# The last routing of a mixture of experts and its first expert chunks, put in another order

## What is computed

```
x = layernorm(x + latent_self_attention(x))        # 16 heads, latent of 72, causal
x = layernorm(x + cross_attention(x, ctx))         # 16 heads of 64, 120 context rows
x = layernorm(x + experts(x) + shared_ffn(x))

scores = softmax(x @ gate_w.T)                     # 16 experts
topk_w, topk_idx = top_k(scores per sequence and expert, cap = 32)
x_tok = x[topk_idx]                                # gather
h = gelu(x_tok @ Wg.T) * (x_tok @ Wu.T)            # per expert, 256 -> 512
out[topk_idx] += (h @ Wd.T) * topk_w               # 512 -> 256, scatter-add
```

## Time and profile before

| what | value |
|---|---|
| runs | 3175.33, 3177.28, 3179.11 us, median 3177.28 |
| profiled execution: span from first to last instruction | 3171.4 us |
| median of the runs less that span | 5.9 us |
| busy share of the span: PE, DVE, ACT, POOL | 97%, 71%, 68%, 50% |
| first transposes of gathered rows, first expert block | 2294 us, 2298 us |
| begin of chunk 2, of chunk 3 | 2350 us, 2367 us |

### The profile page before, as it was taken

How to read it: one execution, slowest core, us unless ns; L and a number is a source line. 1 busy time by engine, 2 the same in 40 slices (tenths; PEclk the granted TensorE clock), 3 DMA queues, 4 the chain that set the end, 5 groups by cost and what they waited for, 6 DMA issues and landing times. The chain is left out here.

```text
span 3171.4 us, 78666 instructions
## 1 busy us (share of the span) xinstructions
PE 3088.7 (97%) x22624; PEld 2900.2 (91%) x22624; DVE 2256.1 (71%) x6566; ACT 2142.4 (68%) x6930; POOL 1581.9 (50%) x2904
## 2 busy tenths in 40 slices
PE   6999999999999998999999999999989999999998
PEld 5999999999999987999999999999868888889998
DVE  6777777777877877778877778787745455544665
ACT  6888888888887877787877877777734444442222
POOL 3666766766676765333333333333446666653000
PEclk8999999999999999999999999999989999999999
DMA  6444444444444440121111111111245444533333
GB/s 181 117 120 125 127 125 121 121 120 122 127 111 111 125 143 24 48 64 45 54 55 45 57 55 44 64 45 48 94 118 119 100 98 101 128 56 85 120 124 106
DMA packets 193684, 300.70 MB, mean 95 GB/s; under 512 B 33856, under 2 KB 134080, under 8 KB 192704
## 3 DMA queue, kind: packets, MB, share of 16 engines
q1 hardware_dynamic: 168768, 262.91, 27.8%
q0 software_dynamic: 24576, 33.57, 6.2%
HBM read 116.02 MB, written 67.11 MB: 58 GB/s over the span
## 5 line engine op out<-in xcount | busy, mean ns | idle before, releaser
L964 POOL TENSOR_SCALAR ca_prob<-ca_prob,ca_inverse 128x120 f32<-128x120 f32 x1024 | 354.6, 365 | 632.5 <-DVE ca_inverse L1268 630.5
L665 ACT ACTIVATE sa_prob<-sa_prob,sa_shift 128x128 f32<-128x128 f32 (+1 forms) x1024 | 453.6, 461 | 2.6 <-DVE sa_shift L718 2.6
L1206 ACT ACTIVATE ca_prob<-bank,ca_shift 128x120 f32<-128x120 f32 x1024 | 353.7, 366 | 6.0 <-DVE ca_shift L1262 3.5
L460 POOL TENSOR_SCALAR sa_prob<-sa_prob,sa_inverse 128x128 f32<-128x128 f32 x512 | 198.5, 388 | 234.5 <-DVE sa_inverse L726 220.4
L718 DVE CUSTOM_DVE_ANT_0 sa_prob<-bank,sa_mask 128x128 f32<-128x128 f32 (+1 forms) x1024 | 304.7, 352 | 6.9 <-PE bank L138 2.7
L136 PE MATMUL bank<-sa_ow,sa_y_hi 128*128 128x256 f32 x1024 | 279.6, 304 | 0.0
L136 PE MATMUL bank<-sa_kvT_a,sa_q 128*128 128x128 f32 (+1 forms) x1024 | 251.7, 281 | 17.7 <-DMA sa_q<-sa_q_tile 17.4
L138 PE MATMUL bank<-sa_kvT_b,sa_q 112*128 112x128 f32 (+1 forms) x1024 | 261.6, 281 | 0.0
L749 DVE TENSOR_TENSOR sa_pT_lo<-bank,sa_pT_hi 128x384 fp32r<-128x384 f32 x512 | 258.3, 544 | 1.8 <-ACT sa_pT_hi L650 1.8
L138 PE MATMUL bank<-sa_ow,sa_y_lo 112*128 112x256 f32 x1024 | 258.8, 283 | 0.0
L462 POOL TENSOR_SCALAR sa_prob<-sa_prob,sa_inverse 128x256 f32<-128x256 f32 x512 | 244.9, 478 | 0.0
(11 more groups left out here) (259 smaller groups left out, 12014.1 us busy)
## 6 DMA issues: line engine op xcount, KB each, us to landing
sa_q<-sa_q_tile SPq DMA_DIRECT2D x128, 288.0 KB
sa_q<-sa_q_tile SPq DMA_DIRECT2D x160, 112.0 KB
mid_x2T<-ca_x2T SPq DMA_DIRECT2D x32, 512.0 KB, 3.0
ex_sx<-mid_x2T SPq DMA_DIRECT2D x32, 512.0 KB, 3.3
sa_q<-sa_q_tile SPq DMA_DIRECT2D x304, 32.0 KB, 3.0
sa_xT_raw<-in_xT SPq DMA_DIRECT2D x32, 256.0 KB, 2.8
sa_q<-sa_q_tile SPq DMA_DIRECT2D x32, 256.0 KB
sa_x_res<-in_x SPq DMA_DIRECT2D x32, 256.0 KB, 2.8
```

Of the source, the lines that this page charges most:

```text
L460: pool.tensor_scalar(prob[:, r, hh, 0:P], prob[:, r, hh, 0:P], inverse[:, r, 2 * hh:2 * hh + 1], 1.0, ALU.mult, ALU.mult)
L665: act.activation(prob[:, r, hh, cols], prob[:, r, hh, cols], ACT.Exp, bias=shift[:, r, n:n + 1], scale=-1.0, accum_out=total[:, r, n:n + 1 ...
L964: ins = pool.tensor_scalar(prob[:, r, t, hh], prob[:, r, t, hh], inverse[:, r, n:n + 1], 1.0, ALU.mult, ALU.mult)
L1206: act.activation(prob[:, r, t, hh], SC[g % 2][:, n * S:n * S + S], ACT.Exp, bias=shift[:, r, n:n + 1], accum_out=total[:, r, n:n + 1]).the ...
```

## The change

Three things change. In the table, chunk 0's rows move from step 8 to 7, its blocks from 10 to 13 to steps 11, 12, 13 and 15 (one block between two routing steps), chunk 1's rows from 14 to 12, and chunk 0's down product from 14 to 22, behind the score transposes. Of chunk 1's blocks one is at step 31 (before: three at 29 to 31), the other three stand behind the columns of step 46, followed by the down product of chunk 1 with the rows of chunk 2 in its middle. Chunk 2's blocks get a line of their own (47), with the rows of chunk 3 between its second and third block; before, these rows came behind the fourth, and the rows of chunk 2 behind the whole down product.

Second, for chunks 0 and 1 the down product is made in two halves, DOWN (hidden blocks 0 and 1) and DOWN_END (2 and 3), each over all four token tiles, and each hidden block is waited for by itself. Third, GpSimd gathers chunk 0's rows one tile in each of steps 0 to 3 (before: four at step 5) and chunk 1's four tiles at step 5, ahead of the subtractions of step 6 (before: at step 10).

```
-    W0_HI, X0_IN, W1_IN, W1_HI, W1_LO, X1_IN, W1_DOWN = (4, 5, 6), 5, 2, (7, 8, 9), 6, 10, 12
+    W0_HI, X0_IN, W1_IN, W1_HI, W1_LO, X1_IN, W1_DOWN = (4, 5, 6), (0, 1, 2, 3), 2, (7, 8, 9), 6, 5, 12
...
-            if isinstance(J, int) and J == BODIES and m == X0_IN:
-                pool.wait_ge(v_mm, 2 * B)
...
-                gather_ahead(0)
+            if isinstance(J, int) and J == BODIES and m in X0_IN:
+                if m == X0_IN[0]:
+                    pool.wait_ge(v_mm, 2 * B)
...
+                gather_ahead(0, (X0_IN.index(m),))
+            if isinstance(J, int) and J == BODIES and m == X1_IN:
+                gather_ahead(1)
             if isinstance(J, int) and J == BODIES and m == W1_LO:
...
-            if isinstance(J, int) and J == BODIES and m == X1_IN:
-                gather_ahead(1)
...
-EXPERTS_AT = {8: ((0, ROWS),), 10: ((1, 0),), 11: ((1, 1),), 12: ((1, 2),), 13: ((1, 3), (1, LAST)), 14: ((1, ROWS), (1, DOWN)),
...
+DOWN_END = EVICT + 1
+EXPERTS_AT = {7: ((0, ROWS),), 11: ((1, 0),), 12: ((1, ROWS), (1, 1)), 13: ((1, 2),), 15: ((1, 3), (1, LAST)), 22: ((1, DOWN), (1, DOWN_END)),
...
-            if f == DOWN:
+            if f in (DOWN, DOWN_END) and isinstance(J, int) and J == 0:
+                down_half(downs(J, m), f == DOWN_END)
+            elif f == DOWN:
                 down(J, downs(J, m))
...
+        def down_half(n, second):
+            if exists(0, n):
+                i, (e, _) = n % 2, of_chunk(0, n)
+                if not second:
+                    if n == 0:
+                        need(pe, xlo_done, n_of(0, 1))
+                    split_done(0, n, 1)
+                    need(pe, act_out, n_of(0, n - 1))
+                    need(pe, dve_out, n_of(0, n - 1))
+                wd = weights(w_hi, e, WD, C), weights(w_lo, e, WD, C)
+                for f in range(FT // 2, FT) if second else range(FT // 2):
+                    need(pe, hlo_done, n_of(0, n, FT, f - FT + 1))
+                    for t in range(CHUNK // P):
+                        ts = slice(t * P, t * P + P)
+                        to = DB[t // 2][:, (t % 2) * C:(t % 2) * C + C]
+                        mm = three(pe, to, h_hi[:, i, f, ts], h_lo[:, i, f, ts], wd[0][:, f], wd[1][:, f],
+                                   f == 0 and t % 2 == 0, f == FT - 1)
+                        if f == FT - 1 and t % 2:
+                            mm.then_inc(d_mm.own, 1)
```

More of the change, by code:

```diff
@@ L947, in first_values, with gather_ahead @@
                           allow_small_or_imprecise_dtypes=True).then_inc(first_done, 1)
-        def gather_ahead(e):
-            for t in range(TILES):
+        def gather_ahead(e, tiles=range(TILES)):
+            for t in tiles:
                 pool.indirect_dma_start(first.x_raw[:, e, t], None, d["x2"][0:SEQS * TILES].rearrange("b t c -> (b t) c"),
@@ L969, in slot @@
                 pool.tensor_tensor(rstd[:], var_eps[:], half[:], ALU.pow).then_inc(rstd_done, 1)
-            if isinstance(J, int) and J == BODIES and m == X0_IN:
-                pool.wait_ge(v_mm, 2 * B)
[L972 to L975, removed]
-                gather_ahead(0)
+            if isinstance(J, int) and J == BODIES and m in X0_IN:
+                if m == X0_IN[0]:
+                    pool.wait_ge(v_mm, 2 * B)
+                    pool.wait_ge(k_mm, B // 2 * NP)
+                    pool.wait_ge(col_done, TILES)
+                    for i in range(2):
+                        pool.wait_ge(x2_out[i], 32 * (SEQS * TILES // 2))
+                gather_ahead(0, (X0_IN.index(m),))
+            if isinstance(J, int) and J == BODIES and m == X1_IN:
+                gather_ahead(1)
             if isinstance(J, int) and J == BODIES and m == W1_LO:
@@ L1402 @@
 PARTS_OF_CHUNK = range(EVICT + 1)
-EXPERTS_AT = {8: ((0, ROWS),), 10: ((1, 0),), 11: ((1, 1),), 12: ((1, 2),), 13: ((1, 3), (1, LAST)), 14: ((1, ROWS), (1, DOWN)),
-              29: ((2, 0),), 30: ((2, 1),), 31: ((2, 2),), 46: ((1, EVICT), (2, 3), (2, LAST), (2, DOWN), (2, EVICT))}
+DOWN_END = EVICT + 1
+EXPERTS_AT = {7: ((0, ROWS),), 11: ((1, 0),), 12: ((1, ROWS), (1, 1)), 13: ((1, 2),), 15: ((1, 3), (1, LAST)), 22: ((1, DOWN), (1, DOWN_END)),
+              31: ((2, 0),), 46: ((1, EVICT), (2, 1), (2, 2), (2, 3), (2, LAST), (2, DOWN), (2, ROWS), (2, DOWN_END), (2, EVICT)),
+              47: ((3, 0), (3, 1), (3, ROWS), (3, 2), (3, 3), (3, LAST), (3, DOWN), (3, EVICT))}
 EXPERTS_AHEAD = {at for parts in EXPERTS_AT.values() for at in parts}
@@ L1746, in down @@
                 i, (e, _) = n % 2, of_chunk(J, n)
-                if isinstance(J, int) and J == 0 and n == 0:
-                    need(pe, xlo_done, n_of(J, 1))
                 split_done(J, n, 1)
```

## The result

| kernel | runs | median | ratio to the kernel before, 95% interval |
|---|---|---|---|
| before | 5 | 3177.28 us | |
| after | 5 | 3156.41 us (3154.9 to 3158.19) | 0.9939 (0.9928 to 0.995) |

The change gains 0.6%, or 20.9 us between the medians; 3160.5 was predicted, with 3155 to 3170 as the range. The span of the profiled execution fell from 3171.4 to 3155.1 us, that is by 16.3. What the change touches can be measured more sharply than the whole: I take the passage from the transposes of the probabilities two pairs ahead of the last ones to the transposes of the fifth chunk's rows. The first fence has its two ends in TensorE's timeline before, the second the waits between them after (start, duration, engine, line, operation, idle time before it and what ended it).

The account below looks back on a forecast made before the run. TensorE was taken as the bound, losing 23.2 us to waits and low clock ahead of the experts. Less new waits and 1.5 of low clock, 16.7 gained: 3177.3 falls to 3160.6, stated as 3160.5 us, range 3155 to 3170.

Parts of the forecast that it names:

- last probabilities later, low clock with it: End of cross attention: gathers on GpSimd delay the probabilities by 0.5 us; one remaining low-clock stretch of TensorE costs 1.5.
- eviction of chunk 0's rows: Behind chunk 0's gather: eviction takes 2.6 us, two output projections cover 1.4, leaving a wait of 1.2 us.
- last norm: Ahead of the transposes of x2: norm done 3.6 us after block 0's start, block 0 takes 2.8; wait 1.0 us.
- scores: Score transposes: about 4.8 us remain from block 2's end, 3.2 covered; wait 1.6 us, ends 0 and 3.5.
- indices: Selection of indices: 7.2 us, beside chunk 0's down product and one block; wait 0.7 us, ends 0 and 2.2.
- What goes: Between cross attention and experts: seven TensorE waits, 16.7 us, plus 6.5 lost to low clock; 23.2 us could be won.
- rivals: Longer and cold waits, 3167 us, chance 0.19; waits only move, 3174, 0.08; slower through GpSimd's queue, 3184.6, 0.04.
- longer and cold: Rival: four low-clock stretches instead of one, chunk 2's gather 2 us late; 10 us gained, 3167 us, chance 0.19.
- signs that were named: In the trace: prediction wrong if probabilities come over 2 us later; chunk 2's first block straight behind the down product's second half.
- Gathers among the probabilities: GpSimd's queue: 1.0 to 1.3 us put ahead of the probabilities, partly covered by ScalarE's exponentials; cost 0.5, ends 0 and 12.
- eviction of chunk 2's rows: Ahead of chunk 2: its 2.54 us lies beside the down product's second half of 2.9; wait nothing, at most 0.4.
- "around the span": Profiled span 3171.4 us against the runs' median 3177.3: 5.9 us taken to lie around it; gain applied to the median.

Follow-up runs that it names:

- second profile: The changed kernel run and profiled a second time, unchanged: passage 81.9 us, median 3156.94 us, ratio 0.9941 to the kernel before.
- the gathers at 0, 1, 4, 4: Changed kernel with the third and fourth gather of chunk 0 moved from steps 2 and 3 to step 4: 3158.2 us, ratio 0.9949.
- the norm first: Changed kernel with chunk 0's gathers at steps 0, 1, 4, 4 and GpSimd's four subtractions moved behind the last norm: 3154.79 and 3155.55 us.
- covered evictions alone: Kernel before with only the rows of chunks 2 and 3 moved, down products of chunks 0 and 1 in halves: 3171.47 us, ratio 0.9985.

## Why the prediction was right, and where it was not

| term | predicted | after | second profile |
|---|---|---|---|
| last probabilities later, low clock with it | 0.5 + 1.5 | 1.94 | 0.65 |
| eviction of chunk 0's rows | 1.2 | 1.18 | 1.18 |
| last norm | 1.0 | 0.94 | 0.94 |
| scores | 1.6 | 0.96 | 0.97 |
| indices | 0.7 | 0.77 | 0.75 |
| ahead of chunk 2 | 0 | 0.90 | 1.12 |
| sum | 6.5 | 6.69 | 5.61 |
| gain: 23.2 less the sum; measured | 16.7 | 16.5; 17.2 | 17.6; 18.3 |

The first row is the time from the passage's start to the last probabilities' transposes, 8.25 and 6.96 us, less 6.31 before (2279.44 to 2285.75). The 0.7 us between the last row's two numbers are the same in both profiles and not assigned.

**What goes** was right: 23.2 us of waits and low clock were there to be won, and none of the rivals came. The first rival's "longer and cold" would have needed four stretches and the gather of chunk 2 two microseconds late; there was one stretch, or none, and no wait for that gather. Of the signs that were named, the probabilities came near their limit (1.94 of 2 us late), and the first block of chunk 2 stood 0.90 us behind the down product instead of straight behind it.

**Gathers among the probabilities** came out at 0.65 us for 0.5 where no low clock is mixed in, and in the way forecast: "ScalarE's exponentials, which run beside it, cover part". On GpSimd the gather and its issue held the probabilities in full, since these were ready when the root was (1.34 us behind the root's end instead of 0.06), and TensorE's wait for them grew from 0.44 to 1.62 in every profile with a gather there, in none with it moved. But without it TensorE stood again ahead of the last probabilities (0.38 us before, 0.57 with the gathers at 0, 1, 4, 4) for the split of the context product, whose high part stands behind those exponentials on ScalarE's queue; behind the 1.62 that wait is gone. So the last probabilities came 6.95 to 7.03 us behind the passage's start in the four profiles with a gather there and no low clock, and 6.30 to 7.95 in the eight without it, by the length of ScalarE's stall: the same gather costs 0.65 beside the stall of 1.75 and next to nothing beside one of 2.45. The clock was the part that missed: "The first two, with transposes between, resemble the 1.63 and 1.88 that preceded the first low stretch" chose the wrong place. The low stretch came earlier, behind the 1.62, and in two of six profiles with that wait; so the 2.0 us taken for both terms together agree with the first profile by luck, and the second has 0.65.

**Scores** were overestimated by 0.6 us, and the **eviction of chunk 2's rows** was the one step that failed: "2.54 lies beside the second half of the down product (2.9)", it said, and costs "nothing, at most 0.4". It began 1.5 us behind the recorded end of the transposes for a cause that stays open, and cost 0.9. In the sum the two nearly cancel.

**The last norm** came out right by luck, for a reason that the prediction did not have. "GpSimd comes to it about as early as before" is true to 0.2 us (20.0 us behind the passage's start, 20.2 before), but the 2.20 of idle that stood ahead of the root were taken for room in hand. The subtractions had used them up: they waited 2.05 for ScalarE, ended 0.1 ahead of the root, and held VectorE's add (0.67 us). Without that hold, with the norm first, the wait is 0.44 and not the 1.0 of the forecast. The gathers at 0, 1, 4, 4 showed that the subtractions were now the bound.

**The time itself** lay 4.1 us under the forecast though the gain in the passage was off by 0.5 (1.6 in the second profile). The 5.9 us "around the span" were wrong: after, the profiled run took 3157.21 us for a span of 3155.1, that is 2.1. With the same 2.1 the profiled execution before took 3173.5, 3.8 below the median from which the gain was taken.

## What to carry to other kernels

A chain that must be hidden is worth its parts only together: earlier gathers alone gave nothing and covered evictions alone a fifth, since each move uncovers the next link, while the whole change without the earlier gathers lost half of its gain. When an instruction is put into an in-order queue ahead of work that is ready, count it in full on that queue, and then look at the next wait of the bounding engine, which may give part of it back: here 1.2 us of wait became 0.65. And before an instruction is moved away from there, look for what it kept apart, here a norm and four subtractions. For a change of some ten microseconds in three thousand, measure the stretch that it touches between two marks in the trace, and compare the profiled execution's own time with the runs before its gain is taken off their median.

## What the runs showed of the hardware

- VectorE's add of 128x2 values took 0.17 us alone, 0.67 and 2.94 beside GpSimd's four subtractions of 128x512 (5.0 us together), and both times ended with the last of them; in the 2.94 two boundaries between these subtractions passed (at about 2296.9 and 2298.1) without its getting through. The statistics that VectorE made beside them kept their 0.75. The Trainium skill, SBUF — State Buffer, SBUF: two separate sides, says that GpSimd and some VectorE operations share a port pair which one holds for a whole instruction while the other stands; the runs agree, and here it was held over several.
- The same wait of 1.62 us was followed by a granted clock of 0.51 in one profile of a kernel and by 1.00 in another of the same kernel; those two passages differ by 1.1 us.
- A gather's rows were there 1.8 us behind its last issue with little else under way, 5.1 us behind it with stores and weights in transfer.
- Halves of the down product, which change the PSUM region at every third matmul instead of every twelfth, kept their 0.12 us a matmul.
